# Adding two images of a 1x1-convolution residual on GpSimd in place of four through a unit matrix on TensorE, and a denser schedule of the finishing instructions

## What is computed

```python
def _L1_conv_ref(x, W, b):
    x_denoised = median_blur(x, 3)                                   # 3x3 median, per channel
    y = jnp.einsum('bchw,oc->bohw', x_denoised, W) + b[None, :, None, None]
    return x + y                                                     # x is x1 here
```

## Time and profile before

| what | value |
|---|---|
| median of 3 runs | 418.46 us |
| the three runs | 416.7, 418.46, 418.57 us |
| the profiled execution, its time | 418.77 us |
| its span, first to last instruction | 416.3 us |
| PE, DVE, ACT, POOL busy, share of the span | 97%, 89%, 38%, 46% |
| mean granted TensorE clock | 0.996 of full speed |

### The profile page before, as it was taken

One profiled execution on the slowest core, in us unless ns is written; L12 is line 12 of the kernel. 1 busy time (PEld: TensorE's weight loads), 2 busy tenths in 40 slices (PEclk: granted clock), 3 DMA queues, 4 the chain that ended last, 5 costly groups with the idle time before them and its releaser, 6 DMA issues.

```text
span 416.3 us, 3679 instructions
## 1 busy us (share of the span) xinstructions
PE 402.1 (97%) x1142; PEld 213.1 (51%) x1142; DVE 371.4 (89%) x528; ACT 157.3 (38%) x352; POOL 192.2 (46%) x196
## 2 busy tenths in 40 slices
PE   7889999999999999999999999999999999997994
PEld 2334578956444444444444444444446688843441
DVE  2899866999849999999999998989898999988995
ACT  1466663422253432323232323141413322373861
POOL 3999386531715543435554443434343440032341
PEclk9999999999999999999999999999999999999998
DMA  7980110010101011010101010100100000003654
GB/s 282 418 333 3 47 54 2 9 41 0 53 0 50 1 50 30 22 50 0 50 2 51 0 50 3 50 14 37 39 13 2 0 0 2 0 0 151 252 211 193
DMA packets 7794, 26.70 MB, mean 64 GB/s; under 512 B 992, under 2 KB 1248, under 8 KB 7776
## 3 DMA queue, kind: packets, MB, share of 16 engines
q1 hardware_dynamic: 7776, 26.48, 16.7%
HBM read 18.09 MB, written 8.39 MB: 64 GB/s over the span
## 4 chain that ended last, share of the span: by engine, by line
PE 86%; DVE 7%; ACT 2%; issue 2%; DMA 1%; POOL 1%; SPq 0%; POOLq 0%; DVEq 0%; ACTq 0%
PE conv_ps L380 75%; PE conv_ps L469 4%; PE one_ps L362 4%; PE one_ps L445 2%; PE conv_ps L472 1%; DVE z L660 1%; DVE z L661 1%; DVE stats L666 1%; DMA z<-x 1%; DVE y L914 1%; POOL y L339 1%; ACT z L622 1%; ACT sorted_cols L503 0%; ACT y L627 0%; ACT y L630 0%
## 5 line engine op out<-in xcount | busy, mean ns | idle before, releaser
L380 PE MATMUL conv_ps<-ru,wt 128*128 128x512 f32 (+1 forms) x360 | 131.2, 500 | 0.0
L380 PEld LDWEIGHTS conv_ps<-ru,wt 128*128 128x128 f32 x360 | 68.2, 190 | 53.3 <-issue 50.2
L380 PE MATMUL conv_ps<-xu,wt 128*128 128x496 f32 (+3 forms) x240 | 87.4, 500 | 0.0
L573 ACT ACTIVATE y<-conv_ps,sgn 128x512 f32<-128x512 f32 (+1 forms) x40 | 25.5, 637 | 161.5 <-PE conv_ps L380 161.5
L380 PEld LDWEIGHTS conv_ps<-xu,wt 128*128 128x128 f32 x240 | 45.5, 190 | 35.4 <-issue 33.2
L313 POOL TENSOR_TENSOR ru<-eo 128x512 f32<-128x512 f32 x16 | 17.0, 1061 | 86.5 <-DVE one_ps L781 86.3
L221 POOL TENSOR_TENSOR ru<-z 128x512 f32<-128x512 f32 x14 | 18.0, 1289 | 59.5 <-DVE one_ps L823 59.5
L380 PE MATMUL conv_ps<-ru,v 128*128 128x496 f32 (+3 forms) x120 | 43.7, 500 | 0.0
L380 PE MATMUL conv_ps<-y,v 128*128 128x496 f32 (+3 forms) x108 | 38.6, 491 | 0.0
L380 PE MATMUL conv_ps<-y,wt 128*128 128x496 f32 (+3 forms) x108 | 38.6, 491 | 0.0
L469 PE MATMUL conv_ps<-z,w 128*128 128x512 f32 x64 | 31.3, 624 | 5.7 <-DVE y L914 3.4
(11 more groups left out here) (127 smaller groups left out, 663.9 us busy)
## 6 DMA issues: line engine op xcount, KB each, us to landing
z<-x SPq DMA_DIRECT2D x16, 512.0 KB, 10.5
raw<-x SPq DMA_DIRECT2D x16, 512.0 KB, 3.3
out<-y SPq DMA_DIRECT2D x15, 512.0 KB, 2.6
wt<-w_t SPq DMA_DIRECT2D x2, 576.0 KB, 10.0
out<-y SPq DMA_DIRECT2D x2, 256.0 KB, 2.0
w<-w_t SPq DMA_DIRECT2D x2, 64.0 KB, 7.9
vec<-vectors SPq DMA_DIRECT2D x1, 3.0 KB, 9.1
```

The source lines that it names most:

```text
L380: return nc.tensor.matmul(bank(u, b)[:, (r0 - row) * BW:(r1 - row) * BW], taps(half, kx, ky), plane[:, (r0 + dy) * BW:(r1 + dy) * BW], sta ...
L573: S.activation(at(slot(n), row * W + b, [[2, cols]]), src, ACT.Identity, scale=sgn[:, :], accum_out=y_sum[:, part:part + 1]).then_inc(y_ke ...
```

## The change

`SUMMED` becomes (4, 9). For these two images ACT copies the mix from PSUM, with the bias, into the image's own slot of `z` (the median there has been read by then), which frees the PSUM half; POOL adds `z` to the normalised slot in `y`, three images later in its own order, and signals the transfer out. The unit matrix, its products and its making are gone. OWN has 14 images in place of 12. The batch norm goes behind count 9 instead of 7, and the finishes at counts 13, 16, ... 43, eleven of them instead of nine.

```diff
--- before.py
+++ after.py
@@ -46,10 +46,10 @@
     BY_POOL = tuple(n for n in range(IMAGES) if n not in BY_DVE)
 
 
-    SUMMED = (3, 6, 9, 12)
+    SUMMED = (4, 9)
     OWN = [n for n in range(IMAGES) if n not in SUMMED]
 
-    BN3_AT, FINISH_AT = 7, (16, 19, 22, 25, 28, 31, 34, 37, 40)
+    BN3_AT, FINISH_AT = 9, (13, 16, 19, 22, 25, 28, 31, 34, 37, 40, 43)
 
 
     HALVED = (0, 1, IMAGES - 2, IMAGES - 1)
@@ -90,7 +90,6 @@
         v1 = sb("v1", [CH, 2 * KY * CH])
         w1 = sb("w1", [CH, CH])
         w2 = sb("w2", [CH, CH])
-        unit = sb("unit", [CH, CH])
         p_kept = [sb(f"p_kept{k}", [CH, BANK]) for k in range(2)]
         sorted_cols = sb("sorted_cols", [CH, 3 * COLS])
         col_lo, col_mid, col_hi = (sorted_cols[:, k * COLS:(k + 1) * COLS] for k in range(3))
@@ -181,9 +180,8 @@
         warm = sem("warm")
         med_ready = sem("med_ready")
         mix_done = sem("mix_done")
-        ones_set = sem("ones_set")
-        unit_made = sem("unit_made")
-        out_by_act = sem("out_by_act")
+        mix_kept = sem("mix_kept")
+        out_by_pool = sem("out_by_pool")
         out_ready = sem("out_ready")
         out_sent = sem("out_sent")
 
@@ -244,7 +242,7 @@
                 sp.dma_start(raw[n % 2][:, :], x_img[:, n, :]).then_inc(raw_in[n % 2], 16)
             for n in range(IMAGES - 1):
                 if n in SUMMED:
-                    sp.wait_ge(out_by_act, SUMMED.index(n) + 1)
+                    sp.wait_ge(out_by_pool, SUMMED.index(n) + 1)
                 else:
                     sp.wait_ge(out_ready, OWN.index(n) + 1)
                 sp.dma_start(out_img[:, n, :], slot(n)).then_inc(out_sent, 16)
@@ -330,11 +328,6 @@
                 make_ru03(n)
                 make_xu03(n)
 
-            G.memset(unit[:, :], 1.0).then_inc(ones_set, 1)
-            pool.wait_ge(ones_set, 1)
-            G.affine_select(out=unit[:, :], in_=unit[:, :], pattern=[[-1, CH]], base=0, channel_multiplier=1,
-                            compare_op=ALU.is_equal, fill=0.0).then_inc(unit_made, 1)
-
             def map_x1(n):
                 G.tensor_scalar(slot(n), slot(n), scale3[:, :], shift3_bias2[:, :], ALU.mult, ALU.add).then_inc(x1_by_pool, 1)
 
@@ -348,6 +341,10 @@
                 G.memset(at(zslot(n), 0, [[(H - 1) * W, 2], [W - 1, 2]]), 0.0).then_inc(med_ready, 1)
                 if n in OWN:
                     map_x1(n)
+                if n - 3 in SUMMED:
+                    pool.wait_ge(x1_by_act, SUMMED.index(n - 3) + 1)
+                    pool.wait_ge(mix_kept, SUMMED.index(n - 3) + 1)
+                    G.tensor_tensor(slot(n - 3), slot(n - 3), zslot(n - 3), ALU.add).then_inc(out_by_pool, 1)
 
         @block.tensor
         def _(pe):
@@ -466,10 +463,7 @@
                     if n == 0:
                         pe.wait_ge(half_ready, b + 1)
                     half = slice(b * BANK, (b + 1) * BANK)
-                    mm = nc.tensor.matmul(conv_ps[:, k, half], w2[:, :], zslot(n)[:, half], start=True, stop=n in OWN)
-                    if n in SUMMED:
-                        pe.wait_ge(x1_by_act, SUMMED.index(n) + 1)
-                        mm = nc.tensor.matmul(conv_ps[:, k, half], unit[:, :], slot(n)[:, half], start=False, stop=True)
+                    mm = nc.tensor.matmul(conv_ps[:, k, half], w2[:, :], zslot(n)[:, half], start=True, stop=True)
                     if b == 1 or n == IMAGES - 1:
                         mm.then_inc(mix_done, 1)
 
@@ -478,13 +472,12 @@
             for _ in range(KEEP_WARM):
                 nc.tensor.matmul(conv_ps[:, other, 0:BANK], zeros[:, 0:CH], zeros[:, :], start=True, stop=True)
             pe.wait_ge(w2_in, 16)
-            pe.wait_ge(unit_made, 1)
             pe.wait_ge(squares_summed, PARTS_ALL)
             for n in range(2):
                 mix(n, n)
             for n in range(2, IMAGES):
                 if n - 2 in SUMMED:
-                    pe.wait_ge(out_by_act, SUMMED.index(n - 2) + 1)
+                    pe.wait_ge(mix_kept, SUMMED.index(n - 2) + 1)
                 else:
                     pe.wait_ge(out_ready, OWN.index(n - 2) + 1)
                 mix(n, n % 2)
@@ -627,7 +620,7 @@
                     S.activation(slot(n), slot(n), ACT.Relu, bias=shift3[:, :], scale=scale3[:, :]).then_inc(x1_by_act, 1)
                 if n - 2 in SUMMED:
                     act.wait_ge(mix_done, n - 1)
-                    S.activation(slot(n - 2), conv_ps[:, n % 2, :], ACT.Identity, bias=cb2).then_inc(out_by_act, 1)
+                    S.activation(zslot(n - 2), conv_ps[:, n % 2, :], ACT.Identity, bias=cb2).then_inc(mix_kept, 1)
 
         @block.vector
         def _(dve):
```

## The result

| | before | after |
|---|---|---|
| median of 7 runs | 418.46 us | 420.9 us |
| lowest, highest | 416.66, 418.86 us | 419.9, 421.36 us |
| profiled execution, its time | 418.77 us | 421.36 us |
| its span | 416.3 us | 419.0 us |

The ratio is 1.0073, with an interval of 1.0051 to 1.0094: the change costs some 0.7%. The medians lie 2.4 us apart; measured again on another chip, the changed kernel lay 3.8 us above the kernel before (420.0 against 416.21). The executions of one kernel spread by up to 2 us here, for reasons that the experiments settle only in part.

A forecast was written before the change was run, and what follows sets the result against it. The prediction took the end as set by when DVE is through with its three pieces of median and what is threaded into them; its parts summed to +1.4 us, giving 419.9 us against the median, range 417.0 to 421.8.

The forecast's parts named there:

- 2, batch norm without a wait: Batch norm behind count 9: two median steps of 1.33 us fill DVE's wait of 1.11 us before it, -1.11.
- 3, no late mixes through the unit matrix: Unit-matrix products leave PE: DVE's waits of 1.88, 0.64 and 0.62 us before three finishes go, -3.14.
- 4, map and L781: L781 no longer loses 0.67 us beside a POOL map; a map of image 5 costs it 0.17 instead: -0.50.
- 5, finish of image 0: DVE reaches the early first finish at 370.63, but its mix allows a start only at 372.3: new wait, +1.70.
- 6, finishes of images 5 and 10: DVE waits before these finishes because their mixes need the finishes of images 3 and 8: +0.70 and +0.36.
- Part 8: ACT loses normalisations and copies, POOL gains maps; transfers of images 4 to 6 wait some 2 us, clear long before the end.
- Part 7: POOL's additions, 2.0 us each, holding DVE's two-SBUF-operand instructions: +1.00 for image 9 (bounds 0 and 2.0), nothing for image 4.
- POOL wins the tie: Rival: image 4's addition starts just before DVE's L823, which stands for the whole 2.0 us; 421.9 us, chance 0.17.
- Part 9: Last mix on PE stays at the lower clock, 3.6 us; between 0 and -1.7, taken as 0.
- last mix at the full clock: Rival: the last mix on PE runs at full clock, 1.7 us less than forecast; 418.2 us, chance 0.25.
- rival on the lower clock: Rival: PE falls to the lower clock earlier, mixes take 3.6 us, each image up to 0.4 more; 422.5 us, chance 0.05.
- No new waits: Rival: finishes 0, 5 and 10 in time and no port meeting, so parts 5 to 7 (-3.8) fall away; 416.1 us, chance 0.13.

The follow-up runs named there:

- delayed kernel: Three one-column memsets on POOL ahead of image 4's addition, delaying it by 0.1 us, against the changed kernel: 419.53 us, ratio 1.0065.
- held-back kernels: The changed kernel with both POOL additions waiting until DVE has passed its two-SBUF-operand instruction: 418.66 us with batch norm at count 9, 418.58 us at 7.

## Why the time came within the range, with two parts wrong

It said 419.9 us with 417.0 to 421.8; 420.9 came, within the range, but over the half per cent (420.6) that I had taken for no change, so "slower" (0.28) came and not "within" (0.60). The point lay only 1.0 us off because two errors of opposite sign stood in it, and that is luck: the parts gave +1.4 where DVE's stretch grew by 4.53, and with a last mix of 3.6 us, as forecast, the time would have been some 422.5, outside the range.

| part | predicted | measured in the profile after |
|---|---|---|
| 1, two finishes | +2.38 | +2.4 (399.80 to 401.00 is one) |
| 2, batch norm without a wait | -1.11 | -1.11 |
| 3, no late mixes through the unit matrix | -3.14 | -3.14, those waits are gone |
| 4, map and L781 | -0.50 | -0.61 (L774 now costs 0.36, L781 cost 0.97) |
| 5, finish of image 0 | +1.70 | +1.78 |
| 6, finishes of images 5 and 10 | +0.70, +0.36 | +0.76, +0.40 |
| 7, addition of image 9 | +1.00 | +1.96 (2.33 - 0.37) |
| 7, addition of image 4 | 0 | +2.18 (2.48 - 0.30) |
| 9, last mix | 0 | -1.64 |

Parts 1 to 7 as measured sum to +4.62; the stretch grew by 4.53. Part 8, nothing from the transfers, held: the span ends 2.4 us behind the last finish both times.

- **Parts 1 to 6 were right**, each wait in its place and all within about 0.1 us. They came from distances between starts and from one chain for each wait. Part 2 was right as an entry, but it is no gain of its own: with the norm at 7 the stretch is the same, so parts 2 and 5 are one term of +0.6 to +0.7.
- **Part 7 failed, twice.** "For image 4 the same count gives a tie [...] At the tie in rows 6 and 7 DVE won, so nothing here": the rule I drew from one row, that DVE wins a tie, isn't one. POOL won here with a lead of 0.05 us and DVE in the delayed kernel with 0.04. The row used was of a map; maps with a lead of up to 0.09 lost, the addition with 0.05 didn't. And my two starts of "5.5" were good to a tenth at best, so between a price of 0 and one of 2.0 the place of the tie should have carried half the chance, not 0.17. The second failure was the size: "L781 lost 0.67 of the 0.82 [...] by that share it is 1.0". DVE was held for the whole addition and ended 0.25 and 0.33 us behind it, so no share was to be taken off, and the addition was 2.35 us and not 2.0. It also began 0.6 us later behind the finish of image 8 than I had summed (4.36 us from start to start, not 3.77), because mix 9 ran at the lower clock; in the changed kernel's repetition it was 4.01. The rival "POOL wins the tie" (0.17) had its mechanism right and its price, 2.0, nearly.
- The Trainium skill ("SBUF — State Buffer", section on its two sides), with its exclusive port pair for a whole instruction, gave 1.3 for image 9, and the traces agree with it rather than with my share: DVE's instructions, which alone take 0.39 and 0.46 us, ended at 388.57 and 403.42, behind additions that ended at 388.32 and 403.09.
- The Trainium skill's "GPSIMD Engine Reference" gives 4497 ns for an addition of 2048 columns (section 3.1, "Elementwise"; the advice against it stands in 4.1). That led to an estimate of 2.25 us for the addition, 0.1 under the 2.35 measured. My 2.0, from two shorter rows, was the worse one.
- **Part 9 failed the other way.** "this is nearest to the row of 2.28": the idle time before the last mix does not decide its clock. After 2.31 us it ran in 1.96, before the change after 2.28 in 3.60. The kernel before itself seems to have both kinds of execution, to judge by its mean clocks, so the right entry was a chance for each execution and not 0. What decides it is not known. The rival "last mix at the full clock" (0.25) came true, together with the one on the tie: 421.9 - 1.7 = 420.2 would have been their common time, 0.7 under the median.
- **The rival on the lower clock** (0.05) was half right. The clock fell twice in the middle of the stage, but the slowed mixes (2.73 and 2.69 us; 5.40 for two) ended ahead of every finish. "No new waits" fell with the three waits.
- My list of signs held for the batch norm, the three waits and the long DVE instruction, of which there were two; the addition took 2.35 us and not 2.0, the last median instruction ended at 412.1 and not at 409.2, and the last mix was the sign against me that I had named.

Two things stay open. The share of executions with a lower mean clock differs between chips or sessions (before: 8 of 28, 15 of 35 and 5 of 13, while in the first comparison most lay above 418), and I can't say why. And three of the twelve runs without the additions took 419.7 to 420.9 us, two of them at a mean clock of 0.996 and one at 0.999; nothing in the one trace explains 3 us.

## What to carry to other kernels

Before work with two SBUF operands goes to POOL, list DVE's instructions that read two SBUF operands too, and see to it that none is due while POOL's runs: the price is what the first of the two still has to run, it is shown as busy time and not as a wait, and a shift of 0.1 us decides who pays. Hold the offloaded instruction back with a semaphore from behind that place rather than trust a schedule; that alone took 3.6 us off the stretch here. But look at what waits for it in turn: with image 9 late, the transfers at the end gave 0.9 us back. And when the last product after an idle time is on the path, look at several executions before its duration is put into a sum.

## What the hardware showed that I had not expected

- An addition of 128 x 1024 float32 on POOL holds a DVE instruction with two SBUF operands fully: 2.56 us for 224 columns, 2.42 for 288. If DVE is first, POOL loses 0.24 us. DVE instructions with an operand in PSUM ran beside it at their usual length (a finish in 1.27 us, one of 448 columns in 0.64). The maps, with one input, hold DVE likewise (0.91 and 1.10 us for 288 columns) when they lead by 0.38 us or more, and gave way with a lead of 0.09 and less.
- TensorE's clock at the last mix varies between kernels that differ little there: 3.60 us after 2.28 of idle time, 2.65 and 2.69 after 2.47, 1.95 and 1.96 also after 2.47 (the held-back kernels with the norm at 7 and at 9, and the delayed one). What differs is when the granted clock falls: ahead of the mix, within it (1.00 from 409.3 to 410.4 and 0.50 from 410.5 to 412 in the kernel without additions), or behind it. The time of PE's last idle stretch doesn't tell which.
- Within one execution of the changed kernel the granted clock stayed at 1.00 for most of the stage and fell in two places, behind idle times of PE of 3.26 and 2.86 us.
